# Moving two tiles' Gelu rows in one set of DMAs, and scatter-adding whole rows, in a mixture-of-experts kernel

## What is computed

```python
def _L1_cond_ref(x, t_emb, router_W, router_bias, w1, w3, w2, W1e, W2e):
    ...
    shared = jax.nn.silu(xf @ w1) * (xf @ w3) @ w2
    s = jax.nn.sigmoid((jnp.concatenate([xf, tf], axis=-1) @ router_W).astype(jnp.float32))
    sel_scores = s + router_bias
    _, topk_idx = jax.lax.top_k(sel_scores, K)
    ...
    h = jax.nn.gelu(jnp.einsum('nc,ech->enh', xf, W1e), approximate=False)
    y = jnp.einsum('enh,ehc->enc', h, W2e)
    routed = jnp.einsum('ne,enc->nc', combine, y)
    return ((shared + routed) / (N_SHARED + K)).reshape(Bb, Tt, C)
x = x + _L0_cond_ref(x, cond_1024, L0_cond_weight)
x = x + _L1_cond_ref(x, cond_1024, L1_cond_router_W, ...)
```

## Time and profile before

| | us |
|---|---|
| median of 3 runs (1090.34 to 1093.66) | 1090.85 |
| the profiled execution | 1096.81 |
| its span | 1095.0 |
| span up to the first expert product | 647.3 |
| last first product ends | 1062.6 |
| last matmul ends | 1077.1 |

### The profile page before, as it was taken

How to read it: one execution, slowest core, us unless ns; L and a number is a source line. 1 busy time by engine, 2 the same in 40 slices (tenths; PEclk the granted TensorE clock), 3 DMA queues, 4 the chain that set the end, 5 groups by cost and what they waited for, 6 DMA issues and landing times.

```text
span 1095.0 us, 14421 instructions
## 1 busy us (share of the span) xinstructions
PE 1036.6 (95%) x4692; PEld 839.7 (77%) x4692; DVE 509.7 (47%) x824; ACT 293.2 (27%) x461; POOL 350.3 (32%) x320
## 2 busy tenths in 40 slices
PE   6999999999999999999999988979999999999993
PEld 5888778888888888888888876767777777777872
DVE  4555466677332433332322134545555555555642
ACT  3222252332322222222111122223332233233330
POOL 2000000001124434433314001346664454554666
PEclk9999999999999999999999999989999999999997
DMA  4667587768768776778525459978779999999764
GB/s 175 195 217 236 199 287 251 264 227 227 291 211 270 238 274 216 249 255 266 209 49 200 61 171 282 296 172 155 140 147 239 206 218 221 228 225 198 142 119 58
DMA packets 172714, 226.77 MB, mean 207 GB/s; under 512 B 29984, under 2 KB 137888, under 8 KB 163552
## 3 DMA queue, kind: packets, MB, share of 16 engines
q1 hardware_dynamic: 59168, 142.22, 39.8%
q0 software_dynamic: 35024, 46.28, 20.7%
q10 hardware_dynamic: 78464, 37.51, 14.3%
HBM read 111.01 MB, written 96.54 MB: 190 GB/s over the span
## 4 chain that ended last, share of the span: by engine, by line
PE 85%; DMA 7%; DVE 3%; issue 3%; ACT 1%; SPq 0%; POOLq 0%; POOL 0%; DVEq 0%
PE banks L525 11%; PE banks L527 10%; PE banks L526 10%; PE banks L464 10%; PE banks L463 10%; PE banks L465 10%; DMA we<-we_d 5%; PE banks L477 5%; PE banks L478 5%; PE banks L479 5%; PE banks L411 3%; PE banks L412 3%; PE banks L413 3%; DMA out<-ys,row 1%; PE banks L443 1%
## 5 line engine op out<-in xcount | busy, mean ns | idle before, releaser
L1168 POOL DMA_INDIRECT out<-ys,row x142 | 226.2, 1593 | 260.7 <-DMA out<-ys,row 137.2
L463 PE MATMUL banks<-xh,w13h 128*128 128x512 f32 x512 | 200.1, 391 | 1.8 <-DVE xl L732 1.8
L465 PE MATMUL banks<-xh,w13l 128*128 128x512 f32 x512 | 199.9, 390 | 0.0
L464 PE MATMUL banks<-xl,w13h 128*128 128x512 f32 x512 | 199.8, 390 | 0.0
L800 DVE SCALAR_TENSOR_TENSOR gm<-sil,banks 128x512 f32<-128x512 f32 x64 | 43.9, 687 | 252.1 <-ACT sil L606 252.1
L525 PE MATMUL banks<-we,xgth 128*128 x284 | 115.1, 405 | 17.5 <-issue 12.4
L606 ACT ACTIVATE sil<-banks 128x512 f32<-128x512 f32 x64 | 38.2, 597 | 320.9 <-PE banks L465 320.9
L525 PE MATMUL banks<-we,hidth 128*128 x284 | 113.2, 399 | 8.0 <-issue 7.8
L463 PEld LDWEIGHTS banks<-xh,w13h 128*128 128x128 f32 x512 | 96.6, 189 | 22.6 <-issue 2.3
L526 PE MATMUL banks<-we,xgth 128*128 x284 | 112.2, 395 | 0.0
L527 PE MATMUL banks<-we,xgtl 128*128 x284 | 112.2, 395 | 0.0
(11 more groups left out here) (156 smaller groups left out, 1462.2 us busy)
## 6 DMA issues: line engine op xcount, KB each, us to landing
we_d<-ehl SPq DMA_DIRECT2D x32, 1024.0 KB, 7.1
hturn<-hid ACTq DMA_DIRECT2D x284, 64.0 KB
xg<-xs_d ACTq DMA_DIRECT2D x136, 128.0 KB
eraw<-expert_w SPq DMA_DIRECT2D x32, 512.0 KB
we<-we_d SPq DMA_DIRECT2D x8, 2048.0 KB
we<-we_d SPq DMA_DIRECT2D x32, 512.0 KB
x1t_d<-x1t SPq DMA_DIRECT2D x8, 1024.0 KB, 8.8
xin<-x1t_d SPq DMA_DIRECT2D x8, 1024.0 KB, 9.5
```

Of the source, the lines that this page charges most:

```text
L463: pe.matmul(ps[hc % 2][:, :], w_hi, xh[:, j, c, :], start=(c == 0), stop=False)
L464: pe.matmul(ps[hc % 2][:, :], w_hi, xl[:, j, c, :], start=False, stop=False)
L465: last = pe.matmul(ps[hc % 2][:, :], w_lo, xh[:, j, c, :], start=False, stop=(c == DC - 1))
L1168: pool.indirect_dma_start(out_half, IO(row2[:, h, t:t + 1], 0), ys[:, t % RING, h * D // 2:(h + 1) * D // 2], None, compute_op=ALU.add).th ...
```

## The change

- `TURN_LAG` goes from 2 to 3 and with it `LAG` from 3 to 4.
- `hturn` holds two buffers of two tiles; ScalarE moves in odd iterations (and for the last tile, 70, alone) two tiles' Gelu rows by four DMAs of 128 KB. The pieces within a DMA are as before 512 bytes; there are twice as many.
- The wait for `output` goes from iteration 0 to 1, ahead of the first move.
- GpSimd adds whole rows, one DMA of 128 rows of 2 KB a tile, at the token numbers that `slot` holds. `added` now counts tiles of either parity. Scatter t waits for scatter t - 2; where tile t - 1 has another expert, or t is not among the used tiles, for scatter t - 1 too, and otherwise for t - 3, which has landed by then. Which of the two comes out of a table `wait_for` that VectorE fills once in iteration 1 by seven small operations on one partition, and GpSimd loads one value of it per tile into a register.
- `take_y(t)` waits for scatter t - 4 alone.

```diff
-TURN_LAG = 2
+TURN_LAG = 3
 LAG = TURN_LAG + 1
...
-        hturn = sb("hturn", [RING, SUB, P], FP32, 160)
+        hturn = sb("hturn", [2, SUB, PAIR, P], FP32, 160)
...
-            def move_h(t):
-
-                act.wait_ge(hid_done, t + 1 + 2)
+            def move_h(m):
+
+                n = min(PAIR, TILES - m * PAIR)
+                act.wait_ge(hid_done, m * PAIR + n + 2)
                 for g in range(P // Q):
-                    act.dma_start(hturn[g * Q:(g + 1) * Q, t % RING], hid[:, t % RING, g * P:(g + 1) * P]).then_inc(h_moved[t % RING], 16)
+                    act.dma_start(hturn[g * Q:(g + 1) * Q, m % 2, :, 0:n], hid[:, m % 2 * PAIR:m % 2 * PAIR + n, g * P:(g + 1) * P]).then_inc(h_moved[m % 2], 16)
...
-                    if t == 0:
+                    if t == 1:
                         act.wait_ge(o_done, SUB * NBLK)
-                    move_h(t)
+                    if t % PAIR == PAIR - 1 or t == TILES - 1:
+                        move_h(t // PAIR)
...
                 if t >= RING:
-                    for h in range(2):
-                        dve.wait_ge(added[h], 16 * (t + 1 - RING))
+                    dve.wait_ge(added[t % 2], 16 * ((t - RING) // 2 + 1))
...
+            def scatter_waits():
+
+                at, used = cst[0:1, C_TIX:C_TIX + TILES], e8[0:1, 1, E - 1:E]
+                then(dve.tensor_scalar(wait_for[0:1, :], at, 1.0, None, ALU.add))
+                then(dve.tensor_scalar(wait_for[0:1, :], wait_for[0:1, :], 1, 255, ALU.logical_shift_right, ALU.bitwise_and))
+                then(dve.tensor_tensor(same[0:1, 1:TILES], turn_of[0:1, 1:TILES], turn_of[0:1, 0:TILES - 1], ALU.is_equal))
+                then(dve.tensor_scalar(tail[0:1, :], at, used, None, ALU.is_lt))
...
             def scatter(t):
 
+                if t > 1:
+                    pool.wait_ge(added[t % 2], 16 * (t // 2))
+                if 0 < t < 3:
+                    pool.wait_ge(added[(t - 1) % 2], 16)
+                elif t:
+                    landed = pool.value_load(wait_for[0:1, t:t + 1], min_val=16, max_val=16 * (TILES // 2 + 2))
+                    pool.wait_ge(added[(t - 1) % 2], landed)
+                    pool.sem_inc(scatter_free, 1)
                 pool.wait_ge(ys_done, t + 1 + 2)
-                for h in range(2):
-                    if t:
-                        pool.wait_ge(added[h], 16 * t)
-                    pool.indirect_dma_start(out_half, IO(row2[:, h, t:t + 1], 0), ys[:, t % RING, h * D // 2:(h + 1) * D // 2], None,
-                                            compute_op=ALU.add).then_inc(added[h], 16)
+                pool.indirect_dma_start(out[:, :], IO(slot[:, t, 0:1], 0), ys[:, t % RING, :], None,
+                                        compute_op=ALU.add).then_inc(added[t % 2], 16)
```

More of the change, by code:

```diff
@@ L109, in shared_moe_kernel @@
         xgt = sb("xgt", [2, DC, P], FP32, 192)
-        row2 = sb("row2", [2, PADDED], INT32, 196)
+        wait_for = sb("wait_for", [TILES], INT32, 196)
+        same = sb("same", [TILES], INT32, 196.5)
+        tail = sb("tail", [TILES], INT32, 197)
         x1tok = sb("x1tok", [BLK // Q, DC, Q], FP32, 168)
@@ L219, in shared_moe_kernel @@
         xgt_done, hid_done, hidt_done = sem("xgt_done"), sem("hid_done"), sem("hidt_done")
-        h_moved = [sem(f"h_moved{k}") for k in range(RING)]
+        h_moved = [sem(f"h_moved{k}") for k in range(2)]
         ys_done = sem("ys_done")
-        halved = sem("halved")
-        added = [sem(f"added{h}") for h in range(2)]
+        waits_done, scatter_free = sem("waits_done"), sem("scatter_free")
+        added = [sem(f"added{j}") for j in range(2)]
         block = ctx.enter_context(nc.Block())
@@ L378, in _ @@
             sp.wait_ge(out_stored, 16 * NBLK)
-            for h in range(2):
-                sp.wait_ge(added[h], 16 * TILES)
+            for j in range(2):
+                sp.wait_ge(added[j], 16 * ((TILES - j + 1) // 2))
         @block.tensor
@@ L1066, in turn_h @@
             def turn_h(t):
-                dve.wait_ge(h_moved[t % RING], 16 * (P // Q) * (t // RING + 1))
+                if t % PAIR == 0:
+                    dve.wait_ge(h_moved[t // PAIR % 2], 16 * (P // Q) * (t // RING + 1))
                 if t >= 2:
@@ L1071, in turn_h @@
                 dve.transpose(hidt[:, t % 2].rearrange("p c (a r) -> p a c r", r=Q),
-                              hturn[:, t % RING].rearrange("p a (c n) -> p a c n", n=Q)).then_inc(hturn_done, 1)
+                              hturn[:, t // PAIR % 2, :, t % PAIR].rearrange("p a (c n) -> p a c n", n=Q)).then_inc(hturn_done, 1)
             def take_h(t):
@@ L1082, in take_y @@
                 if t >= RING:
-                    for h in range(2):
-                        dve.wait_ge(added[h], 16 * (t + 1 - RING))
+                    dve.wait_ge(added[t % 2], 16 * ((t - RING) // 2 + 1))
                 dve.tensor_scalar(ys[:, t % RING, :], y_ps[t % 2][:, :], slot[:, t, 1:2].bitcast(FP32), None, ALU.mult).then_inc(ys_done, 1)
+            def scatter_waits():
[4 more added lines that the diff above has]
+                then(dve.tensor_scalar(tail[0:1, :], at, used, None, ALU.is_lt))
+                then(dve.tensor_tensor(same[0:1, 1:TILES], same[0:1, 1:TILES], tail[0:1, 1:TILES], ALU.mult))
+                then(dve.tensor_tensor(same[0:1, 1:TILES], wait_for[0:1, 1:TILES], same[0:1, 1:TILES], ALU.subtract))
+                dve.tensor_scalar(wait_for[0:1, 1:TILES], same[0:1, 1:TILES], 16.0, None, ALU.mult).then_inc(waits_done, 1)
             turn_x(0)
@@ L1093, in _ @@
                     dve.wait_ge(slots_in, 16 * SUB)
-                    for h in range(2):
-                        dve.tensor_scalar(row2[:, h, :], slot[:, :, 0], 2.0, float(h), ALU.mult, ALU.add).then_inc(halved, 1)
+                    scatter_waits()
                 if t > LAG:
@@ L1158, in _ @@
                         load_row(m + XB)
-            pool.wait_ge(halved, 2)
-            out_half = out.rearrange("t (h d) -> (t h) d", h=2)
+            pool.wait_ge(waits_done, 1)
             def scatter(t):
-                pool.wait_ge(ys_done, t + 1 + 2)
-                for h in range(2):
-                    if t:
-                        pool.wait_ge(added[h], 16 * t)
-                    pool.indirect_dma_start(out_half, IO(row2[:, h, t:t + 1], 0), ys[:, t % RING, h * D // 2:(h + 1) * D // 2], None,
-                                            compute_op=ALU.add).then_inc(added[h], 16)
+                if t > 1:
[6 more added lines that the diff above has]
+                    pool.sem_inc(scatter_free, 1)
+                pool.wait_ge(ys_done, t + 1 + 2)
+                pool.indirect_dma_start(out[:, :], IO(slot[:, t, 0:1], 0), ys[:, t % RING, :], None,
+                                        compute_op=ALU.add).then_inc(added[t % 2], 16)
             pool.wait_ge(out_stored, 16 * NBLK)
```

## The result

The changed kernel takes 1102.72 us (median of 4 runs, 1100.87 to 1103.70), against 1090.59 us for the kernel before beside it (4 runs): ratio 1.0135, 95% interval 1.0099 to 1.0171. It is **slower by 1.35%** by that ratio (the two medians alone are 12.1 us, 1.1%, apart), where the forecast was 1068 us and faster. The profiled execution took 1103.7 us with a span of 1101.8, 1.0 us above its median; that of before was 6 us above its own. So the profiles show 6.8 us of the 12.1 between the medians. Second product 0 is the first matmul that reads `hidth`; "main" runs from there to the end of first product 70.

A forecast was written before the change was run, and what follows sets the result against it. It took TensorE, busy 95%, as bound, held up by ScalarE's slackless queue and scatter waits. Drip 14, stall 8, end 0.4, one product less 2.7, start -2.3: 23 us less, 1068 us from the median; range 1057 to 1084.

The forecast's parts named there:

- The drip is ScalarE's: Expert stage: 22 us of TensorE gaps in 66 tiles come from ScalarE's full queue; the change gains 14 us.
- slack 0.45 us: Odd tile's path from Gelu to hidtl: 4.8 us against 5.28, so a set up to 3.0 us costs nothing.
- 8 us residue: Part of the 22 us drip that stays: long sets, the slow first matmul after each, register loads midway.
- Rival D: Expert stage: register loads and DMA load make the drip, whatever ScalarE's queue holds; 14 us stay, 1082 us; chance 0.07.
- One set of moves: ScalarE's queue: one set for two tiles takes 2.65 us, saving 2.63 us a pair, 11.0 to 8.4.
- A: Rival on ScalarE's moves: a paired set takes 3.1 to 3.3 us, drip stays some 20 us, 1080 us; chance 0.13.
- B: Rival on ScalarE's moves: from 3.7 us a set the gain is gone, 1091 us; at 5.1 us, 1137; chance 0.14.
- One tile later: Start of the expert stage: TURN_LAG 3 puts second product 0 at 673.1 instead of 668.03, loss 2.3 us.
- stall near 720 us: TensorE's one stall, 8.0 us, laid to late scatter landings; two whole-row scatters in flight remove it.
- rival C: Scatters: landing grows with bytes, 22 us for two whole rows in flight; stall stays, 1076, slower end 1083; chance 0.11.
- The end: After first product 70: scatter 66 at 5.4 us, four 5.1 us steps, landing 4.4, then 1.5: 32 us (28 to 38).

The follow-up runs named there:

- single_scatter: The changed kernel with a set of moves for each tile again, whole-row scatters and TURN_LAG 3 kept: 1100.56 us, ratio to before 1.0092.
- dma_last_single: dma_last with a set of moves for each tile instead of each pair: 1070.70 us, ratio to before 0.9823.
- Known_after: The changed kernel with TensorE's turn and place as program constants instead of register loads: 1078.57 us, ratio to before 0.9918.
- lookup_even: The changed kernel with the register loads of the next two tiles made midway in even first products only: 1093.69 us, ratio to before 1.0042.
- dma_last_half: dma_last with the half-row scatters of the kernel before: 1106.08 us, ratio to before 1.0153.
- moves_only: The changed kernel with the half-row scatters of the kernel before, so paired moves and TURN_LAG 3 only: 1098.42 us, ratio to before 1.0134.
- scatter_only: The kernel before with the whole-row scatters alone, moves per tile and TURN_LAG 2 kept: 1090.93 us, ratio to before 1.0046.
- lag_only: The kernel before with TURN_LAG 3 alone: 1090.03 us, ratio to before 1.0019.
- dma_last: The changed kernel with ScalarE's activations first in each iteration and the sets of moves and loads after them: 1068.97 us, ratio to before 0.9833.

## Why the prediction was wrong, point by point

**What bounds the kernel.** "The drip is ScalarE's" was right in part and its arithmetic was not. The prediction added ScalarE's work for a pair (11.0 us) and took off what the change takes off the queue (8.4). But the order in the queue makes a loop, and only what stands on the loop counts: one set of moves and one set of loads, both behind the odd tile's Gelu, and the register loads ahead of the seventh matmul. The path that the prediction did follow, Gelu to `hidtl` (slack 0.45 us), leaves out the other end, from the moves through the loads of x to the next `xgth`. Single moves in place of paired ones (single_scatter, dma_last_single) change the medians by 2 us, beside half rows the pairing cost 8.4 us, and with the DMAs last the 22 us go whether or not the moves are paired. This is the failed step: 2.63 us of queue time taken off for each pair of tiles, summed as 14 us of gain, was worth none, since the set that went was not on the loop. The loop itself grew from 11.61 to 11.84 us.

**The register loads.** They stood in the prediction as one of three makers of an 8 us residue, at no price of their own. They took 13.1 us midway (forecast residue 8 in all), and two things that the change did bear on it: whole-row scatters slow a load from 0.31 to 0.65 us in the mean where they meet, and they meet in odd tiles, whose lead the longer sets cut from 1.13 to 0.64 us. Known_after puts 24 us on them. As a part of the loop they did not grow (2.61 us before, 2.51 after); what grew there are the moves, by 0.30 us, and the loads of x, by 0.12, while ScalarE's waits in it shrank by 0.2. Rival D named them ("register loads and DMA load make it") and gave 1082, at 0.07, as something that stays; that they could grow with the change was in no case. Rival D's evidence against it was one long set followed by one gap, which the loop explains as well.

**One set of moves.** A little under-sized: 2.75 us in the median (2.65 taken), 3.00 in the mean on the loop, and a quarter of the sets at 3.2 us or more, where one in eight above 3.0 was taken. A (3.1 to 3.3) is near in size, B (3.7) is not; but neither alone is the cause, since the kernel with single moves is slower than before by 0.9% too.

**One tile later.** Right: gap of 2.29 us ahead of second product 0 where 2.3 was summed; the start measured 6.0 us more than before where 5.1 was forecast.

**Scatters, stall near 720 us.** The wait for landing went, as forecast; whole rows land in 8 to 9 us beside the weight loads, with two in flight (up to 11.5 in lookup_even and dma_last_single), not the 22 of rival C. The Trainium skill ("DMA: Bandwidth & Descriptors", Queues, rings and completion order) lets queues take turns by packets and not by bytes; by that rule the landing should not have doubled, and the trace agrees with it: the half rows of dma_last_half, also two in flight, take 8 to 10 us there. But the 8 us stayed spent. A set of x loads now takes 6.90 us there, and TensorE stands still for 3.99 us before 702.96 and then runs at a granted clock of 0.50 for one product (6.6 us together). ScalarE, around 700 us:

```profile
694.38 0.63 ACT L692 ACTIVATE hidth<-hidt 128x512 fp32r<-128x512 f32 x1 [3.09 <-PE banks L529]
694.40 6.90 ACTq L664 DMA_DIRECT2D xg<-xs_d  x4
701.40 0.63 ACT L670 ACTIVATE xgth<-xgt 128x512 fp32r<-128x512 f32 x1 [6.39 <-issue]
```

The prediction didn't ask what is late next once the scatter isn't. The DMA engines are full there (share 1.05 from 696 to 703 us), and ScalarE's issue stands on the loop. But they were as full before (1.14), where no set of x loads up to 735 us took over 2.6 us, and moves_only, with half rows, has one of 5.69 us at 695.26. Why this set is so long isn't shown.

**The end.** 36.1 us against 32. Scatter 66 is issued 6.1 us after the last first product (5.4 taken), the four steps take 5.08, 6.06, 5.07 and 5.37 us (4 x 5.1 taken), the landing 4.65 (4.4 taken); together 2 us over. The rest is behind the last landing: 3.8 us to the end of the span where 1.5 was taken. GpSimd's closing row, before and after (ns, start):

```profile
L75 POOLq DRAIN  x1: 5624/5624/5624, 1089.1 to 1089.1; - x1
```
```profile
L75 POOLq DRAIN  x1: 8445/8445/8445, 1093.1 to 1093.1; - x1
```

**The Trainium skill's other rule** ("DMA: Bandwidth & Descriptors", Anatomy of one DMA) gives, for 128 KB more at 436 GB/s, 0.30 us more for a whole row than for a half, an estimate; the prediction's 0.15 was half of that, and its end "some 3 us shorter" would have been some 2. The quiet landings of the last three whole rows are 4.29, 4.58 and 4.65 us against 3.65, 0.6 to 1.0 more; the measurement decides, and the value taken from the rows was the better one.

**The range** (1057 to 1084) missed 1102.72 because all its cases but B took pairing as a relief or, in D, as nothing, and B's price was looked for in the moves alone. The side was lost with the step on the loop. Two things stay open. In the profiles the start costs 3.3 us more than before (6.0 less the product that moved there), main's gaps 5.4 and the end 1.0 (3.7 less a product), and the time ahead of the expert stage, which the change doesn't touch, was 2.8 shorter; with 5 us between profiles and medians this split is no better known than that. And scatters two in flight among the last padding tiles, which would shorten the end, weren't tried.

## What to carry to other kernels

When one engine both issues DMAs and does work on the critical path, don't only add up its time per round: follow one dependence all the way round to itself (here product, Gelu, moves, loads, `xgtl`, product two tiles on), and count what stands on it. Where such a loop is longer than the bottleneck's own round, reorder the queue before making the transfers fewer: putting 4.8 us of issuing behind 1.6 us of activations was worth 34 us, halving the moves gained nothing that could be told, and cost 8 us beside half-row scatters. And when a wait is to be removed, price the small instructions beside it again, at the places where the removed wait's traffic will now stand, and ask which second resource (here half-row scatters behind the register loads) holds the same rate.

## What the runs showed of the hardware

- A register load by TensorE's queue takes 0.30 us in quiet, and 0.65 us in the mean, up to 0.99, when it starts 2 to 3 us after a whole-row scatter-add of 128 rows is issued (in scatter_only 26 such loads take 0.86, up to 1.23). With half rows it is 0.52 (before), 0.49 (lag_only) and 0.44 (moves_only). The scatter-add's own first pieces move 2.3 us after its issue; why they slow the load isn't shown.
- GpSimd's closing drain ends 3.6 us after the last landing in the changed kernel, where the last scatter-add has whole rows, and 1.3 us after it in dma_last_half, where it has half rows. The cause is open; it costs 2.3 us.
- On ScalarE, an instruction that only issues a DMA runs beside the activations that it doesn't depend on: in dma_last the first `hturn` DMA of 0.62 us starts at 900.88 within the `hidth` activation of 900.75, and before the `xgth` activation that stands ahead of it in the list.
